# Two more tile pairs by Strassen's product in a fused embedding, threshold and projection kernel

## What is computed

```python
q_emb = relu(cond @ W3 + b3)                       # (16, 512)
v_sum = sum(x, axis=1, keepdims=True)
y = relu(((256 * x + v_sum) * q_emb[:, None, :]) @ W2 + b2)
x_q = where(y > 0.33, 0.5, 0.0)                    # y is never negative
w_q = where(weight > 0.2, 0.6, where(weight < -0.2, -0.6, 0.0))
out = x + einsum('bsd,od->bso', x_q, w_q + rram_variation)
```

## Time and profile before

| | us |
|---|---|
| median of 3 runs (173.34 to 174.48) | 173.36 |
| the profiled execution | 172.84 |
| its span, first to last instruction | 170.9 |
| TensorE busy in the span | 165.6 (97%) |
| VectorE / ScalarE / GpSimd busy | 131.4 / 67.4 / 85.4 |
| granted TensorE clock | 1.000 |

### The profile page before, as it was taken

How to read it: one execution, slowest core, us unless ns; L and a number is a source line. 1 busy time by engine, 2 the same in 40 slices (tenths; PEclk the granted TensorE clock), 3 DMA queues, 4 the chain that set the end, 5 groups by cost and what they waited for, 6 DMA issues and landing times.

```text
span 170.9 us, 2183 instructions
## 1 busy us (share of the span) xinstructions
PE 165.6 (97%) x684; PEld 122.1 (71%) x684; DVE 131.4 (77%) x196; ACT 67.4 (39%) x173; POOL 85.4 (50%) x85
## 2 busy tenths in 40 slices
PE   7989999999999999999999999999999999999991
PEld 2889987777554578686653459997653559999991
DVE  3589998998998999774968998778736267776751
ACT  2155269936102259999007996432000001001000
POOL 3001950849105592560089302759099203999990
PEclk9999999999999999999999999999999999999999
DMA  5999999999600494729949005983293000353166
GB/s 164 255 245 234 228 214 227 222 216 219 121 0 0 118 358 120 140 64 260 398 120 372 16 0 154 342 308 124 94 341 117 0 4 6 118 195 117 70 251 232
DMA packets 31211, 28.99 MB, mean 170 GB/s; under 512 B 1600, under 2 KB 22368, under 8 KB 31200
## 3 DMA queue, kind: packets, MB, share of 16 engines
q1 hardware_dynamic: 30128, 28.07, 60.4%
q10 hardware_dynamic: 1008, 0.79, 1.5%
q0 software_dynamic: 64, 0.00, 0.0%
HBM read 20.47 MB, written 8.39 MB: 169 GB/s over the span
## 4 chain that ended last, share of the span: by engine, by line
PE 87%; DVE 4%; issue 2%; ACT 0%; DVEq 0%; ACTq 0%
PE out_ps L957 12%; PE hid_ps L957 10%; PE out_ps L934 9%; PE out_ps L1020 8%; PE hid_ps L866 6%; PE hid_ps L859 6%; PE hid_ps L927 6%; PE hid_ps L908 5%; PE hid_ps L920 5%; PE hid_ps L883 5%; PE hid_ps L900 5%; PE hid_ps L1007 5%; PE hid_ps L1012 4%; PE hid_ps L934 2%; DVE xT L532 1%
## 5 line engine op out<-in xcount | busy, mean ns | idle before, releaser
L430 ACT ACTIVATE xT<-xT,coef,q_scale 128x256 f32<-128x256 f32 x64 | 33.9, 592 | 13.2 <-DVE coef L583 7.3
L532 DVE STREAM_TRANSPOSE xT<-x_in 128x1024 f32<-128x1024 f32 x15 | 30.7, 2053 | 0.0
L436 ACT ACTIVATE junk<-xT,q_emb 128x256 bf16<-128x256 f32 x40 | 19.8, 496 | 13.5 <-DVE xT L532 13.4
L370 POOL TENSOR_TENSOR x_res<-x_res,pieces 128x256 f32<-128x256 f32 x8 | 5.9, 734 | 24.2 <-DVE x_res L706 24.2
L486 ACT ACTIVATE pieces<-out_ps 128x256 f32<-128x256 f32 x6 | 2.3, 383 | 31.8 <-PE out_ps L957 29.8
L1020 PE MATMUL out_ps<-xT,w_sb 128*128 128x512 f32 x32 | 14.1, 599 | 0.0
L376 POOL TENSOR_TENSOR x_res<-x_res,pieces 128x256 f32<-128x256 f32 x16 | 13.4, 862 | 0.0
L934 PE MATMUL out_ps<-wT_lo,hid 128*128 128x512 f32 x32 | 13.3, 415 | 0.0
L1020 PEld LDWEIGHTS out_ps<-xT,w_sb 128*128 128x128 f32 x32 | 9.8, 309 | 3.8 <-ACT xT L430 0.2
L934 PE MATMUL out_ps<-wT_hi,hid 128*128 128x512 f32 x32 | 12.5, 390 | 0.0
L359 POOL TENSOR_TENSOR a_sum<-hid 128x1024 fp32r<-128x1024 f32 x2 | 4.7, 2348 | 14.6 <-DVE t_sum L611 14.6
(11 more groups left out here) (134 smaller groups left out, 410.6 us busy)
## 6 DMA issues: line engine op xcount, KB each, us to landing
x_in<-in_x SPq DMA_DIRECT2D x24, 256.0 KB, 5.6
x_res<-in_x SPq DMA_DIRECT2D x3, 2048.0 KB, 9.2
out<-x_res SPq DMA_DIRECT2D x24, 256.0 KB, 3.5
x_in<-in_x SPq DMA_DIRECT2D x1, 2048.0 KB, 9.4
out<-x_in SPq DMA_DIRECT2D x7, 256.0 KB, 2.1
x_in<-in_x SPq DMA_DIRECT2D x12, 128.0 KB, 6.2
w_sb<-in_L_cond_W SPq DMA_DIRECT2D x4, 256.0 KB, 6.0
x_res<-in_L_ffn_weight SPq DMA_DIRECT2D x4, 256.0 KB, 7.1
```

Of the source, the lines that this page charges most:

```text
L430: nc.scalar.activation(part, part, ACT.Identity, bias=coef[:, n, k:k + 1], scale=q_scale[:, n, k:k + 1]).then_inc(s_xs, 1)
L532: nc.vector.transpose(xT[:, s, :, cols].rearrange("p j (n t) -> p n j t", t=BLK), x_in[:, p % SLOTS, b * NB:(b + 1) * NB].rearrange("p n ( ...
```

## The change

- Group 0 is projected directly for tiles 0, 1, 4 and 5 only (`DIRECT`). Tiles 2, 6 and 3, 7 become pairs (0,2) and (0,3). Pairs are numbered by `pair_number(g, c) = 4 * g + c - 2`, so (0,2) is number 0 and (0,3) number 1, and all semaphore counts move with it.
- GpSimd makes the hidden sums of these two pairs, `hidden_sums(0)`, with 256 columns instead of 512, in front of the `wT_lo` subtractions, and calls `add_pieces(0, c)` in front of `hidden_sums(1)`.
- The thresholds of group 0's second half move from VectorE (`quantize(1, m)`) to ScalarE: Sign of the product plus a bias column, then Relu, through a tile `sign`. A column `bias_col` is made on VectorE.
- ScalarE rounds weight sums 0 and 1 before batch 8's sums, 2 and 3 between these sums and the scaling. GpSimd makes `b_lo` in the order 0, 1, 3, 2, and the waits on `s_blo` go to the single part that is used.
- The token sum of batch 11 moves from ScalarE to VectorE (`prepare(11)`), which stands between `pair_u2(0, 3)` and `pair_c21(0, 3)`.
- Pair (0,3) uses `hid_ps`, so p1, p5 and p6 of group 2 now wait for VectorE's additions of that pair (`wait_pair_banks`, before only in the last group).

The diff, cut to its core:

```diff
-    PAIRS_OF = (0, 4, 4, 3)
+    PAIRS_OF = (range(2, 4), range(4), range(4), range(3))
     TILES = 8
+    DIRECT = (0, 1, 4, 5)
-    VECTOR_SUMS = (2, 3, 6, 7)
+    VECTOR_SUMS = (2, 3, 6, 7, 11)
...
+        def pair_number(g, c):
+            return 4 * g + c - 2
...
-            store(0, range(TILES))
+            store(0, DIRECT)
+            store_pairs(0)
...
+            def hidden_sums(g):
+                cols = slice(2 * P, TOK) if g == 0 else slice(0, TOK)
...
+                if g == 0:
+                    pool.wait_ge(s_cls_hid, KD)
+                    pool.wait_ge(s_cls_hid2, KD)
...
+            hidden_sums(0)
             for h, cols in enumerate(COLS):
                 pool.wait_ge(s_whi, h + 1)
...
-            for i in range(4):
+            for i in (0, 1, 3, 2):
                 pool.wait_ge(s_bhi, i + 1)
...
+            for c in PAIRS_OF[0]:
+                add_pieces(0, c)
             pool.wait_ge(s_tsum, 8)
             hidden_sums(1)
...
+            act.wait_ge(s_th, 2)
+            for m in range(KD):
+                act.wait_ge(s_cls, KD + m + 1)
+                if m > 0:
+                    act.wait_ge(s_cls_hid2, m)
+                nc.scalar.activation(sign[:], out_ps[m][:], ACT.Sign, bias=bias_col[:, m:m + 1]).then_inc(s_sign, 1)
+                act.wait_ge(s_sign, m + 1)
+                nc.scalar.activation(hid[:, 0, m, TOK:], sign[:], ACT.Relu).then_inc(s_cls_hid2, 1)
...
-            sum_and_scale(8)
-            sum_and_scale(9)
-            for i in range(4):
...
+            weight_sum_hi(0)
+            weight_sum_hi(1)
+            act.wait_ge(s_tr, 8)
+            accumulate(8)
+            weight_sum_hi(2)
+            weight_sum_hi(3)
+            scale(8)
+            act.wait_ge(s_tr, 9)
+            accumulate(9, (0, 1))
+            copy_pair_p1(0, 2)
+            accumulate(9, (2, 3))
+            scale(9)
+            copy_pair_p1(0, 3)
             sum_and_scale(10)
-            sum_and_scale(11)
+            scale_summed(11)
...
+            nc.vector.tensor_scalar(bias_col[:], b2_col[:], TH_X, None, ALU.subtract).then_inc(s_th, 1)
...
-            quantize(1, 0)
...
-            for m in range(1, KD):
-                quantize(1, m)
...
             finish(0)
             finish(1)
+            c12(1, 1)
             finish(2)
             transpose_batch(10)
             finish(3)
-            c12(1, 1)
-            finish(4)
-            transpose_batch(11)
-            for c in range(5, TILES):
-                finish(c)
+            finish_pair(0, 2)
+            pair_c22(0, 3)
+            pair_u2(0, 3)
+            prepare(11)
+            pair_c21(0, 3)
+            pair_c11(0, 3)
+            pair_c12(0, 3)
+            pair_u3(0, 3)
...
-            def wait_pair_banks(b):
-                pe.wait_ge((s_o21, s_o11, s_o12, s_u3)[b], 4)
+            def wait_pair_banks(g, b):
+                pe.wait_ge((s_o21, s_o11, s_o12, s_u3)[b], pair_number(g - 2, 3) + 1)
...
-                if g == LAST:
-                    wait_pair_banks(j)
+                if g > 1:
+                    wait_pair_banks(g, j)
...
+                pe.wait_ge(s_blo, 1)
+                if u == 0:
+                    pe.wait_ge(s_out, 3)
...
+                if u == 0:
+                    pe.wait_ge(s_out, len(DIRECT))
...
             project(0)
             project(1)
+            p3(1, 1)
             project(2)
             project(3)
-            p3(1, 1)
-            for c in range(4, TILES):
-                project(c)
+            for c in PAIRS_OF[0]:
+                project_pair(0, c)
```

More of the change, by code:

```diff
@@ L127, in adaln_ffn_kernel @@
         th_col = sbuf("th_col", [P, KD])
+        bias_col = sbuf("bias_col", [P, KD])
+        sign = sbuf("sign", [P, TOK])
         warm = sbuf("warm", [P, D], mybir.dt.bfloat16)
@@ L384, in last_hidden_sums @@
                 sums = a_sum[:].bitcast(F32)
-                done = 4 * (LAST - 1 + c)
+                done = 4 * (LAST + c)
                 if c == 0:
@@ L412, in _ @@
             last_hidden_sums(2)
-            for c in range(PAIRS_OF[LAST]):
+            for c in PAIRS_OF[LAST]:
                 add_pieces(LAST, c)
@@ L512, in _ @@
             for g in (2, LAST):
-                for c in range(PAIRS_OF[g]):
+                for c in PAIRS_OF[g]:
                     copy_pair_p1(g, c)
             for h, cols in enumerate(COLS):
-                act.wait_ge(s_out, TILES + 2 + h)
+                act.wait_ge(s_out, len(DIRECT) + 2 + h)
                 act.dma_start(out_tiles[LAST * TILES + TILES - 1, :, cols], res[LAST][:, TILES - 1, cols]
@@ L583, in prepare, with quantize @@
                 nc.vector.tensor_tensor(coef[:, n], x_sum[:], q_emb[:, n], ALU.mult).then_inc(s_coef, 1)
[L585 to L588, removed]
+            def quantize(m):
+                dve.wait_ge(s_cls, m + 1)
+                nc.vector.tensor_scalar(hid[:, 0, m, 0:TOK], hid_ps[m][:], b2_col[:, m:m + 1], TH_X,
                                         ALU.add, ALU.is_gt).then_inc(s_cls_hid, 1)
@@ L665, in c12, with finish @@
                                         ALU.is_gt).then_inc(s_c12, 1)
-            def finish(c):
+            def finish(i):
+                c = DIRECT[i]
                 dve.wait_ge(s_x_res[0], DMA)
-                dve.wait_ge(s_out_ps, c + 1)
-                nc.vector.scalar_tensor_tensor(x_res[:, c], out_ps[c % 4][:], SC_X, x_res[:, c],
+                dve.wait_ge(s_out_ps, i + 1)
+                nc.vector.scalar_tensor_tensor(x_res[:, c], out_ps[i][:], SC_X, x_res[:, c],
                                                ALU.mult, ALU.add).then_inc(s_out, 1)
@@ L715, in pair_u3, with finish_pair @@
                                                ALU.mult, ALU.add).then_inc(s_u3, 1)
-            def finish_pairs(g):
[L718 to L724, removed]
+            def finish_pair(g, c):
+                pair_c22(g, c)
+                pair_u2(g, c)
+                pair_c21(g, c)
+                pair_c11(g, c)
+                pair_c12(g, c)
+                pair_u3(g, c)
+            def finish_pairs(g):
+                for c in PAIRS_OF[g]:
+                    finish_pair(g, c)
             def transpose_weight(h):
@@ L879, in p6 @@
                     pe.wait_ge(s_c12, u)
-                    if g == LAST:
-                        wait_pair_banks(2)
+                    if g > 1:
+                        wait_pair_banks(g, 2)
                 for k in range(2):
@@ L896, in p5 @@
                     pe.wait_ge(s_c12, u - 1)
-                    if g == LAST:
-                        wait_pair_banks(3)
+                    if g > 1:
+                        wait_pair_banks(g, 3)
                 for k in range(2):
@@ L1062, in _ @@
                     project_pair(g - 1, c)
-            for c in range(PAIRS_OF[LAST]):
+            for c in PAIRS_OF[LAST]:
                 project_pair(LAST, c)
-            pe.wait_ge(s_o21, 4 * (LAST - 1) + 2)
+            pe.wait_ge(s_o21, pair_number(LAST, 1) + 1)
             project_part(LAST, 3, hid_ps[0], slice(0, D)).then_inc(s_out_ps, 1)
-            pe.wait_ge(s_o11, 4 * (LAST - 1) + 2)
+            pe.wait_ge(s_o11, pair_number(LAST, 1) + 1)
             project_part(LAST, TILES - 1, hid_ps[1], COLS[0]).then_inc(s_out_ps, 1)
-            pe.wait_ge(s_o12, 4 * (LAST - 1) + 2)
+            pe.wait_ge(s_o12, pair_number(LAST, 1) + 1)
             project_part(LAST, TILES - 1, hid_ps[2], COLS[1]).then_inc(s_out_ps, 1)
```

102 lines of the change are left out of this document (56 added, 46 removed).

## The result

The changed kernel is slower: 176.88 us median of 4 runs (176.02 to 177.43) against 173.35, a ratio of 1.018 (95% interval 1.0135 to 1.023). Two of the four executions had a mean granted clock of 1.00 (176.02 and 176.37 us), two of 0.99 (177.38 and 177.43). The granted clock is TensorE's clock as a share of full speed. The profiled execution took 176.02 us with a span of 173.8; before, 172.84 and 170.9. The forecast was 175.2 in a range of 172.6 to 176.2: right in sign and place, but too small, and the measured time lies above the range.

What follows compares the result with a forecast made beforehand. TensorE was taken to bound the kernel; holes of 2.54 and 0.12 and a 0.07 us bias step, less 0.56 and 0.29, made +1.88 us. Forecast 175.2 us, +1.1%, range 172.6 to 176.2.

Steps and rivals of the forecast that it cites:

- What bounds the kernel: TensorE, busy 165.6 of 170.9 us; a matmul less counts fully, and so does every hole that nothing refills.
- The gain of the pairs: Group 0's projection on TensorE: two pairs at 3.36 us instead of 3.64 each save 0.56 us.
- The covers: Thresholds on ScalarE, hidden and weight sums on GpSimd, and the x_res load are ready before pair (0,2), costed at nothing.
- The first small hole: Fourth product of pair (0,2) writes the bank finish(3) reads, so it slips about 0.12 us.
- The large hole: Before p1(2,0): TensorE waits for pair_c21(0,3), queued behind prepare(11) on VectorE; 2.54 us, bounds 2.2 to 3.2.
- What comes back: ScalarE no longer sums batch 11, so p1(2,0)'s copy is not late and p2(2) gains 0.29 us.
- Sum: All terms, 2.54 + 0.12 + 0.07 - 0.56 - 0.29, give +1.88 us; chance 0.64.
- The range: 172.6 to 176.2 us, from the no-hole rival to the likeliest case's top; likeliest case alone 174.5 to 176.2.
- 1 (VectorE sets group 2's end): VectorE's chain, starting only 0.95 us later, paces group 2 instead of TensorE: 174.3 us; chance 0.12.
- 2 (no hole): pair_c21(0,3) comes early enough for TensorE to go on at once before p1(2,0): 172.7 us; chance 0.10.
- 3 (a table switch): Sign and Relu in different ScalarE tables: 8 loads, 10.2 us, projection 8 us late, about 183 us; chance 0.05.
- 4 (a longer hole): Extra waits inside VectorE's row u2, prepare(11), c21 count in full: 176.2 to 177 us; chance 0.09.

Runs made afterwards that it cites:

- x1: The changed kernel with VectorE's last four additions of pair (0,3) ahead of prepare(11): 178.28 us, ratio 1.025.
- y4: The changed kernel with batch 11's token sum on ScalarE again, VectorE only transposing it between u2(0,3) and c21(0,3): 176.72 us, ratio 1.019.
- x2: As x1, and on ScalarE the two copies of p1(2) ahead of batch 11's scaling: 174.66 us, ratio 1.008.
- z1: The kernel before with only group 0's second-half thresholds on ScalarE and the bias column in VectorE's early row: 173.50 us against 173.53.
- y2: The changed kernel with nine bf16 matmuls, result unread, between the last pair product and p1(2,0): 175.86 us.
- w1: The changed kernel, unedited, run again to count low-clock executions, with a profile that caught one: 177.35 us.
- w3: The changed kernel, unedited, run again for the same count and one more profile, which caught a low clock: 177.74 us.

## Why the prediction was right and where it failed

- **What bounds the kernel.** Right. x1 and y4 move the wait before TensorE or split it, x2 shortens it, and the tail follows each time (113.06, 112.81 and 110.98, against 112.27).
- **The gain of the pairs.** 0.56 us forecast; 0.39 net, since a p1 behind a pair takes 0.12 longer and p2 0.05. The trace of before had a row for the first of these, p1 of group 3 behind pairs, which the sum did not use:

```profile
115.58 3.54 PE hid_ps L859 x8
```

- **The covers.** Thresholds, hidden sums, weight sums, x_res: all hidden. The first three within 1 us of the times given. x_res landed at 66.2 instead of 65.0, inside its 1.5 us of slack.
- **The first small hole.** Forecast 0.12. From the end of the direct tiles (70.56) to the end of pair (0,2) (74.35) the chain takes 3.79 us instead of 3.36, so the hole costs 0.43. That is 0.21 of idling, 0.07 for a slower first matmul (0.35 against 0.28), and 0.16 for the overlap: in an unbroken row a matmul of 0.28 begins every 0.12, and the chain counts only the 0.12; the first one behind a wait counts in full.
- **The large hole.** 2.54 forecast, 2.45 measured, by the row of operations that was named. The stretch from the start of pair (0,3) to p1(2,0) took 5.81 instead of 5.9. From the first projection to p1(2,0) it is 18.63 instead of 18.39: 0.31 for the small hole, less 0.09 here, 0.02 elsewhere.
- **What comes back.** p2(2) takes 3.43 instead of 3.72, the size forecast. z1 has it as well with batch 11's sum where it was, so it does not hang on that sum. But p1(2) takes 3.79 instead of 3.43. Its first matmul behind the wait took 0.79 instead of 0.59, and the other 0.16 is the overlap named above:

```profile
L907 PE MATMUL hid_ps<-xT,w_sb x8: 592/592/790, 80.2 to 83.4; 128*128 128x512 f32 x8
```

- This +0.36 was in no term: the prediction priced a hole by its edges, and the restart costs too. In y2, behind 0.51 us of idling instead of 2.45, p1(2) takes 3.80, so at full clock this price does not grow with the wait.
- **Sum.** Tail: forecast 2.10 - 0.29 = +1.8, measured +2.38. 0.24 up to p1(2,0) and 0.36 in p1(2) are the difference, to within 0.03. Executions at full clock bear it out: the nine of the changed kernel have a median of 175.9, +2.6 on the kernel before, which is 0.7 above the forecast and inside its range.
- **The clock.** This is the step that failed. The sum took a hole of 2.5 us at its length, from a profile where the clock stood at 1.00 throughout, put what the idling does to the clock at nothing without a reason, and gave no rival in which the hole sets the clock down. In 13 of 22 executions the clock was at 0.99, and in the two that were profiled the low clock stands behind the hole and costs 1.4 to 1.6 us. Of the first four executions two had it, at 177.4 us, and the median, 176.88, lies between the two kinds. The two at full clock took 176.02 and 176.37 us, one just inside the range's 176.2 and one just above it. Where in the execution the clock fell in these two is not on record; w1 and w3 show it for the same kernel.
- **The range.** The bounds of the hole, 2.2 to 3.2 us, give 174.9 to 175.9; the 174.5 to 176.2 given are 0.3 to 0.4 wider on each side, and the prediction does not say from what.
- **Rivals.** 1 (VectorE sets group 2's end) fell: the shift of 2.86 us at p1(2,0) is still 2.93 at p3(2,1) (103.10 against 100.17), and x2 against x1 says the same. 2 (no hole) fell. 3 (a table switch) fell: no load but the one at 3.12. The sign named for it, a first projection after 61.3, did come (61.53), but from the w2 load. The list of functions in every set that the Trainium skill gives ("ScalarE: Activation LUTs", "Table sets: the hidden batching unit") leaves out Sign, and here Sign ran between Identity and Relu without a load. 4 (a longer hole) has the measured time in its 176.2 to 177 by luck: the hole was no longer than forecast.

## What to carry to other kernels

A gain of half a microsecond on the bounding engine is lost by one operation of a helper queued in front of the one that frees the bank; look, for every bank that changes hands, at what stands before its last reader. Price a hole on TensorE at its length, plus the slower first matmul behind it, plus the chance of a stretch at the lower clock behind it (here with a hole of 2.4 us), and forecast the median over executions and not the one that was profiled. Compare two variants at the same clock, or by the part of the trace that the edit touches, since a median mixes both kinds. If a hole can't be closed, filling it with matmuls whose result nobody reads took the low clock out here.

## What the hardware showed that was not expected

With a hole of 2.4 us in the work of TensorE, which this kernel otherwise keeps busy from 9 us on, 13 of 22 executions had a mean granted clock of 0.99. In the two of them that were profiled it was 0.50 for about 3 us, from the end of the hole on. With nine bf16 matmuls in the hole (2.1 us) it was 0 of 10. A wait costs more than its length even at full clock: 0.36 us at p1(2), and about as much behind 0.5 us of idling as behind 2.4. The first projection's start varied from 61.0 to 62.5 us from profile to profile, in most of the late ones with the arrival of the w2 loads and in one with a low clock (y4), which is as much as most single edits of this kernel bring.
